# The scan of a time mix run over pairs of tokens instead of single tokens

## What is computed

```python
def step(S, ins):
    r_t, k_t, v_t, w_t = ins
    kv = jnp.einsum('bhi,bhj->bhij', k_t, v_t)
    y_t = jnp.einsum('bhi,bhij->bhj', r_t, S + u[None, :, :, None] * kv)
    return (w_t[..., None] * S + kv, y_t)
...
x = _layernorm(x + time_mix(x))
x = _layernorm(x + experts(x))
```

## Time and profile before

| what | us |
|---|---|
| median of 3 runs (lowest, highest) | 2341.41 (2340.97, 2342.73) |
| profiled execution, its own time | 2343.03 |
| its span | 2341.3 |
| busy: PE, DVE, ACT, POOL | 1938.1, 1834.2, 1059.1, 1373.3 |
| first scan, last scan starts | 65.6, 1274.7 |
| mean granted TensorE clock | 0.922 |

### The profile page before, as it was taken

One profiled execution on the slowest core, in us unless ns is written; L12 is line 12 of the kernel. 1 busy time (PEld: TensorE's weight loads), 2 busy tenths in 40 slices (PEclk: granted clock), 3 DMA queues, 4 the chain that ended last, 5 costly groups with the idle time before them and its releaser, 6 DMA issues. The chain is left out here.

```text
span 2341.3 us, 33041 instructions
## 1 busy us (share of the span) xinstructions
PE 1938.1 (83%) x9894; PEld 1336.8 (57%) x9894; DVE 1834.2 (78%) x3157; ACT 1059.1 (45%) x1919; POOL 1373.3 (59%) x954
## 2 busy tenths in 40 slices
PE   5777888788777887877776299999999999999980
PEld 2333343333333333433332189999999999999970
DVE  2899999899999998999997266666666666666655
ACT  2233553345334543444432255555555555555546
POOL 3667787768777787678775224444444444454440
PEclk9889999899989998999886599999999999999995
DMA  6932111111112111111020144545454545455538
GB/s 163 220 87 64 46 46 54 47 54 36 51 47 58 29 51 42 58 29 49 31 69 20 58 122 121 122 121 120 120 120 122 120 120 121 120 123 122 124 57 287
DMA packets 172844, 209.00 MB, mean 89 GB/s; under 512 B 12796, under 2 KB 152480, under 8 KB 172768
## 3 DMA queue, kind: packets, MB, share of 16 engines
q1 hardware_dynamic: 112688, 143.09, 20.7%
q0 software_dynamic: 28672, 34.78, 8.6%
q10 hardware_dynamic: 31408, 30.33, 5.0%
HBM read 118.65 MB, written 75.53 MB: 83 GB/s over the span
## 5 line engine op out<-in xcount | busy, mean ns | idle before, releaser
L807 DVE TENSOR_TENSOR_SCAN S<-wT,S,vb 128x512 f32<-128x512 f32 x512 | 624.9, 1262 | 0.0
L1070 POOL TENSOR_TENSOR prod<-S,rT 128x2048 f32<-128x2048 f32 x128 | 536.8, 4198 | 148.0 <-DVE S L807 147.8
L1289 PE MATMUL up<-x_parts,w_parts 128*128 128x308 f32 x3072 | 464.2, 307 | 1.5 <-DVE x_parts L1402 1.5
L1304 PE MATMUL down<-w_parts,h_parts 128*128 128x512 f32 (+1 forms) x1280 | 452.4, 396 | 0.0
L1289 PEld LDWEIGHTS up<-x_parts,w_parts 128*128 128x128 f32 x3072 | 439.2, 189 | 4.1 <-issue 1.8
L1364 POOL TENSOR_TENSOR ye<-ye,weight 128x256 f32<-128x256 f32 (+1 forms) x160 | 197.7, 1235 | 379.9 <-DVE ye L1458 379.9
L1342 ACT ACTIVATE h_full<-up,b_now 128x616 f32<-128x616 f32 x256 | 198.6, 776 | 421.2 <-PE up L1289 409.6
L1372 POOL DMA_INDIRECT sums<-ye,sum_at x160 | 281.6, 1760 | 150.1 <-POOL ye L1364 140.0
L1445 DVE TENSOR_TENSOR h_parts<-h_full,h_parts 128x616 fp32r<-128x616 f32 x256 | 206.8, 808 | 193.1 <-ACT h_parts L1342 192.8
L1307 PE MATMUL down<-w_parts,h_parts 128*128 128x256 f32 (+1 forms) x1280 | 357.4, 279 | 0.0
L571 PE MATMUL vb<-v_stack,pick_v 128*128 128x512 f32 x512 | 216.7, 507 | 152.0 <-DVE S L807 151.8
(11 more groups left out here) (176 smaller groups left out, 2645.2 us busy)
## 6 DMA issues: line engine op xcount, KB each, us to landing
w_raw<-in_L_ffn_w_dram SPq DMA_DIRECT2D x64, 1024.0 KB, 8.8
expert_in_rows<-y_tok ACTq DMA_DIRECT2D x30, 652.5 KB, 9.1
xe<-expert_in_rows SPq DMA_DIRECT2D x32, 522.0 KB
v_stack<-v_parts SPq DMA_DIRECT2D x64, 256.0 KB, 4.5
x_tok<-in_L_attn_x_dram SPq DMA_DIRECT2D x16, 512.0 KB, 3.3
x_res<-in_L_attn_x_dram SPq DMA_DIRECT2D x16, 512.0 KB, 3.4
sums<-x_row SPq DMA_DIRECT2D x16, 512.0 KB, 2.9
rows<-sums SPq DMA_DIRECT2D x16, 512.0 KB, 5.5
```

The source lines that it names most:

```text
L807: dve.tensor_tensor_scan(line[:, 1:TC + 1], wT[:, par, half, :], vb[:, p % 2, g, :], line[:, 0:1], ALU.mult, ALU.add).then_inc(scanned, 1)
L1070: pool.tensor_tensor(prod[:, q % 2], S[:, q % RING, :, 0:TC], rT[:, par, half, None, :].to_broadcast([P, QUAD, TC]), ALU.mult).then_inc(pr ...
L1289: last = pe.matmul(up[:, f % 2, half, 0:HC], w1_parts[:, par, wp, k, f * P:(f + 1) * P], x_parts[:, par, xp, k, half * HC:(half + 1) * HC] ...
L1304: pe.matmul(down[0:m, (par * TILES + t) % 2, :, :], h_parts[:, 0, f, t * P:t * P + m], w2_parts[:, par, :, f, :], start=f == 0, stop=False)
```

## The change

The recurrence is run over pairs of tokens. For an even token e and the odd token o behind it, S(o) = w(e) w(o) S + [w(o) k(e) v(e) + k(o) v(o)], so the scan takes 256 steps of w_pair = w(e) w(o), and its input is the sum of two products. The even token's output is r(e) times the state before the pair. The odd token's is r(o) w(e) times the same state, plus a term of its own, r(o) k(e) summed over the head's channels, times v(e). In each chunk the even tokens are put first and the odd ones behind them, in every tile; DMAs of x and x1 read and write the rows in that order, and the counting matmuls keep the order of tokens with a second triangular matrix, `upto`. xp is a new tile that holds, for each token, x of the token before it. `last_norm` puts four neighbouring rows on a partition.

```diff
-              "B0": 27, "B1": 28}
+              "B0": 26, "B1": 27, "D0": 28, "D1": 29}
-        LATER = {"hid": 3, "V": 3, "B": 3}
+        LATER = {"hid": 3, "V": 3, "B": 2, "D": 2}
+        def in_pairs(dram, first):
+            return dram[bass.ds(first, TC), :].rearrange("(l p b) c -> p b l c", p=P, b=2)
...
 @@ PE
+                    if s == AT[f"D{h}"]:
+                        a_fill(i, f"D{h}")
+                        pe.wait_ge(next_done, stage_value(i, 1, 1))
+                        pe.matmul(pa_of(f"D{h}")[:, 0:TP], sum_head[:].rearrange("p j h -> p (j h)"), r_next[:, h, :],
                                   start=True, stop=True).then_inc(a_full, 1)
...
-                    pe.matmul(ypsum[:], ident[:], uT[:, par, half, :], start=False, stop=True).then_inc(y_full, 1)
+                    pe.matmul(ypsum[:], ident[:], uT[:, par, half, :], start=False, stop=False)
+                    wait_drained(pe, i, f"D{half}")
+                    pe.matmul(ypsum[:, TP:TC], ident[:], uT_next[:, par, half, :], start=False, stop=True
+                              ).then_inc(y_full, 1)
...
 @@ DVE
+                    if s == AT[f"D{h}"] + LATER["D"]:
+                        dve.wait_ge(a_full, stage_value(i, NA, FA[f"D{h}"] + 1))
+                        dve.tensor_tensor(uT_next[:, par, h, :], pa_of(f"D{h}")[:, 0:TP], v_full[:, h, 0:TP], ALU.mult
+                                          ).then_inc(drained_sem(f"D{h}"), 1)
...
                     if p == 0:
-                        wait_drained(dve, i, "R1")
-                        dve.wait_ge(w_done, stage_value(i, NH, NH))
-                    for g in range(2):
-                        dve.wait_ge(vb_full, stage_value(i, NU, 2 * p + g + 1))
-                        dve.tensor_tensor(vb[:, p % 2, g, :], vb[:, p % 2, g, :], kT[:, par, half, :], ALU.mult
-                                          ).then_inc(kv_done, 1)
+                        dve.wait_ge(folded, stage_value(i, 3, 3))
+                    dve.wait_ge(vb_full, stage_value(i, NU, 2 * p + 2))
+                    even, odd = vb[:, p % 2, :, 0:TP], vb[:, p % 2, :, TP:TC]
+                    dve.tensor_tensor(kv_even[:], even, kT[:, par, half, None, 0:TP].to_broadcast([P, 2, TP]), ALU.mult
+                                      ).then_inc(kv_done, 1)
+                    dve.tensor_tensor(odd, odd, kT[:, par, half, None, TP:TC].to_broadcast([P, 2, TP]), ALU.mult
+                                      ).then_inc(kv_done, 1)
+                    dve.wait_ge(kv_done, stage_value(i, NU, 2 * p + 2))
+                    dve.tensor_tensor(even, odd, kv_even[:], ALU.add).then_inc(kv_summed, 1)
                     if p % 2 == 0:
                         dve.wait_ge(start_set, stage_value(i, NQ, q + 1))
+                    dve.wait_ge(kv_summed, stage_value(i, NPAIR, p + 1))
                     for g in range(2):
                         line = S[:, q % RING, 2 * (p % 2) + g, :]
-                        dve.wait_ge(kv_done, stage_value(i, NU, 2 * p + g + 1))
-                        dve.tensor_tensor_scan(line[:, 1:TC + 1], wT[:, par, half, :], vb[:, p % 2, g, :],
+                        dve.tensor_tensor_scan(line[:, 1:TP + 1], w_pair[:, par, half, :], vb[:, p % 2, g, 0:TP],
                                                line[:, 0:1], ALU.mult, ALU.add).then_inc(scanned, 1)
...
 @@ ACT
-                        act.activation(xT[:, h, 1:TC + 1], pa_of(f"x{h}"), ACT.Copy).then_inc(drained_sem(f"x{h}"), 1)
+                        now = pa_of(f"x{h}")
+                        act.activation(xp[:, h, TP:TC], now[:, 0:TP], ACT.Copy)
+                        act.activation(xp[:, h, 1:TP], now[:, TP:TC - 1], ACT.Copy)
+                        act.activation(xT[:, h, :], now, ACT.Copy).then_inc(drained_sem(f"x{h}"), 1)
...
 @@ POOL
+                if s == AT["R1"] + 1:
+
+                    pool.wait_ge(rk_done, stage_value(i, NH, NH))
+                    pool.tensor_tensor(r_next[:], rT[:, par, :, TP:TC], kT[:, par, :, 0:TP], ALU.mult
+                                       ).then_inc(next_done, 1)
+                    pool.wait_ge(next_done, stage_value(i, 1, 1))
+                    pool.wait_ge(w_done, stage_value(i, NH, NH))
+                    pool.tensor_tensor(kT[:, par, :, 0:TP], kT[:, par, :, 0:TP], wT[:, par, :, TP:TC], ALU.mult
+                                       ).then_inc(folded, 1)
+                    pool.tensor_tensor(w_pair[:, par], wT[:, par, :, 0:TP], wT[:, par, :, TP:TC], ALU.mult
+                                       ).then_inc(folded, 1)
+                if s == AT["R1"] + 2:
+                    pool.wait_ge(next_done, stage_value(i, 1, 1))
+                    pool.tensor_tensor(rT[:, par, :, TP:TC], rT[:, par, :, TP:TC], wT[:, par, :, 0:TP], ALU.mult
+                                       ).then_inc(folded, 1)
...
-                pool.tensor_tensor(prod[:, q % 2], S[:, q % RING, :, 0:TC],
-                                   rT[:, par, half, None, :].to_broadcast([P, QUAD, TC]), ALU.mult
-                                   ).then_inc(prod_done, 1)
+                pool.tensor_tensor(prod[:, q % 2].rearrange("p g (b s) -> p g b s", b=2),
+                                   S[:, q % RING, :, None, 0:TP].to_broadcast([P, QUAD, 2, TP]),
+                                   rT[:, par, half, :].rearrange("p (b s) -> p b s", b=2)[:, None]
+                                   .to_broadcast([P, QUAD, 2, TP]), ALU.mult).then_inc(prod_done, 1)
...
 @@ last_norm
-            return dram[bass.ds(g * (GT * P) + first, GT * P), :].rearrange("(t p) c -> p t c", p=P)
+            return dram[bass.ds(g * (GT * P) + first, GT * P), :].rearrange("(p t) c -> p t c", t=GT)
```

More of the change, by code:

```diff
@@ L176, in time_mix @@
         uT = sb("uT", [P, 2, NH, TC])
+        w_pair = sb("w_pair", [P, 2, NH, TP])
+        r_next = sb("r_next", [P, NH, TP])
+        uT_next = sb("uT_next", [P, 2, NH, TP])
+        kv_even = sb("kv_even", [P, 2, TP])
         v_parts = sb("v_parts", [P, 2, NH, TC], F32R)
         v_stack = sb("v_stack", [P, 2, NH, 2, TC], F32R)
-        S = sb("S", [P, RING, QUAD, TC + 1])
+        S = sb("S", [P, RING, QUAD, TP + 1])
         carry = sb("carry", [P, NQ, QUAD])
@@ L248, in time_mix @@
         rk_done = sem("rk_done")
+        next_done = sem("next_done")
+        folded = sem("folded")
+        kv_summed = sem("kv_summed")
         vb_full = sem("vb_full")
@@ L461, in stage_a @@
                     for h in range(NH):
-                        pe.matmul(pa_of("hid"), w1_sb[:, h, :], xT[:, h, 1:TC + 1], start=h == 0, stop=False)
+                        pe.matmul(pa_of("hid"), w1_sb[:, h, :], xT[:, h, :], start=h == 0, stop=False)
                     for h in range(NH):
-                        last = pe.matmul(pa_of("hid"), w1_before[:, h, :], xT[:, h, 0:TC], start=False,
+                        last = pe.matmul(pa_of("hid"), w1_before[:, h, :], xp[:, h, :], start=False,
                                          stop=h == NH - 1)
@@ L556, in stage_c @@
                     for t in range(TPC):
-                        pe.matmul(pc[:, t * E:(t + 1) * E], ones[:], seen[:], start=True, stop=False)
-                        for b in range(t):
-                            pe.matmul(pc[:, t * E:(t + 1) * E], ones[:], hits[:, b, :], start=False, stop=False)
-                        last = pe.matmul(pc[:, t * E:(t + 1) * E], before[:], hits[:, t, :], start=False, stop=True)
+                        b, l = t // 2, t % 2
+                        to = pc[:, t * E:(t + 1) * E]
+                        pe.matmul(to, ones[:], seen[:], start=True, stop=False)
+                        for done in range(l):
+                            for side in range(2):
+                                pe.matmul(to, ones[:], hits[:, 2 * side + done, :], start=False, stop=False)
+                        pe.matmul(to, upto[:] if b else before[:], hits[:, l, :], start=False, stop=False)
+                        last = pe.matmul(to, before[:], hits[:, 2 + l, :], start=False, stop=True)
                     last.then_inc(c_full, 1)
@@ L682, in stage_a @@
                     wait_from(dve, a_full, stage_value(i, NA, 0))
-                    dve.tensor_tensor(xx[:], xT[:, :, 0:TC], xT[:, :, 1:TC + 1], ALU.subtract).then_inc(xx_done, 1)
+                    dve.tensor_tensor(xx[:], xp[:], xT[:], ALU.subtract).then_inc(xx_done, 1)
                 for f, n in enumerate(DVE_MIXES):
@@ L1055, in stage_a @@
                                 pool.wait_ge(weighed, stage_value(i, MIX * NH - NSHORT, f * NH + h + 1 - NSHORT))
-                            pool.tensor_tensor(m, m, xT[:, h, 1:TC + 1], ALU.add).then_inc(mixed, 1)
+                            pool.tensor_tensor(m, m, xT[:, h, :], ALU.add).then_inc(mixed, 1)
                 for h in range(NH):
```

34 lines of the change are left out of this document (20 added, 14 removed).

## The result

The changed kernel takes 2397.11 us (median of 4 runs, 2391.85 to 2403.86) against 2341.81 (2340.97 to 2342.73) for the kernel before on the same chip: ratio 1.0238, 95% interval 1.0211 to 1.0264. It is 2.4% slower, where 2344 us was forecast within 2308 to 2372. The profiled execution has a span of 2396.2 us, 54.9 above that of before. The first rows are from the page of the changed kernel: its busy times, then its groups (busy, mean ns | idle before).

What follows compares the result with a forecast made beforehand. GpSimd was taken to hold stretch A in six chunks and a three-engine loop to end stretch B, VectorE not bounding alone. Chunk gains and losses, prologue +5 and end -0.5 summed to +2.5 us: 2344 us, range 2308 to 2372.

Steps and rivals of the forecast that it cites:

- hidden in the 6.75 us that GpSimd idles before the product of group 7: GpSimd's four added 128x512 products a chunk, 1.27 us each, 5.1 us together, were to cost nothing in its idle time.
- the slower rival on the product's own price: GpSimd's product of S and r gets dearer with half lines, up to 0.9 us each; say 2365 us; chance 0.15.
- stretch A: Chunk 2, last scans to first K matmul, 208.0 to 239.3 (31.3 us); set by GpSimd in six chunks, no gain there.
- the chunks after a branch: Chunks 5, 7, 9, 11, 13: VectorE sets stretch A, with 3.4 us of room; it gains 1.7 us there.
- Pair: VectorE's two products, their sum and two 256-step scans take 3.30 us instead of 3.54, saving 0.24 us.
- B0's drain: Moved ahead of pair 14, which then waits for spread, B0 and uT product: 2.3 us instead of 0.5, +1.75 us.
- stretch C: Chunk 2, spread of pair 14 to last scan's end, 271.4 to 282.8 (11.4 us); forecast +1.6 us.
- D0's and D1's drains: VectorE's new drains of the D matmuls; D0's beside B1's in front of pair 15; +0.36 us each.
- Prologue +5: Before the first scan: VectorE waits for the fourth fold, +3.3 us, and ScalarE's copies add 1.6: +5 us.
- Chunk 0: VectorE sets this chunk; 16 x 0.24 us saved, less two D drains: -3 us.
- Chunk 15: VectorE sets this chunk; forecast -3.8 us.
- two signs of being wrong: Last scans of two chunks under 74 us apart on the whole, or the product's mean over 4.3 us.

Runs made afterwards that it cites:

- The pair alone: Kernel before with only the changed kernel's VectorE pair (w in place of w_pair) and its product of S and r: 2331.92 us, ratio 0.997.
- the best variant: Changed kernel with group 6's product behind the top-2 chain, D matmuls late, xT shifted one word and folds by halves: 2355.63 us, ratio 1.0067.

## Why the prediction was wrong

**The step that failed:** "They stand between the second r*k product and the product of group 6, and are hidden in the 6.75 us that GpSimd idles before the product of group 7." GpSimd's idle time did take them: its wait before group 7 is down from 6.75 to 5.45 us in chunk 2. It was forecast to be nearly gone; it stayed because VectorE had become later itself. But I had asked only who waits for GpSimd's results, not what runs on VectorE while the product runs. Moved by 5.1 us, the product of group 6 covered the top-2 chain. That is +28.5 us by the run that takes only this away, and +60 by the run that adds only this to the kernel before. No rival had it; the slower rival on the product's own price had the right engine and the wrong quantity, since the mean stayed at 4.19 us.

**A second step failed by a smaller sum:** the x additions, which I took at their old price without naming them as touched. They cost 0.18 us more each; the run with x shifted is 9 us faster.

Point by point:
- That GpSimd holds stretch A in six chunks: right. After the change K starts 0.05 to 0.15 us behind GpSimd's additions in all eight, and with scans of half the length it still stands at 30.9 us in chunk 8. That it stands at 31.0 there both before and after is luck, as said above: chunks 2, 3 and 4 show 0.7 to 0.9 us more. In the chunks after a branch K moved from 32.9 to 33.9 us up to 32.0, 0.8 to 1.9 us where 1.7 was forecast.
- Pair: 0.24 us saved was forecast, and chunk 15 shows one pair every 3.41 us (1271.37 to 1274.78), so 0.13. Of the 0.11 us between the forecast pair of 3.30 and this, 0.05 are the two scans (0.735, taken at 0.71) and the rest gaps around the sum. The pair alone brings 9 us.
- B0's drain, +1.75 us in stretch C: right in size (1.6 in chunk 8). D0's and D1's drains, priced at 0.36 us: 0.33 each. For the D matmuls' wait for B's drain I had no term; TensorE stood 70.0 us in 14 chunks for it. Half of that was the hold again (35.5 us with the product behind the chain), and VectorE waited only 5.9 us for spreads, so most of it cost nothing. The run with D's matmuls late puts this wait and B0's drain together at 8 us once the hold is gone, not at 14 times 1.75: without the drain pair 14 waits for its spread.
- Prologue +5: VectorE's first product starts at 70.40 us in place of 64.36, +6.0. The second r*k product ends 2.8 us later, where I had 1.6 for ScalarE's copies; the four folds take the forecast 5.1, and the D drains are done 2 us before them. Chunk 0 from there: -1.1 where -3 was forecast. Chunk 15: -3.8 forecast, -0.1 found, as its pair saves half and VectorE waited 2.4 us for spreads.
- I had named two signs of being wrong: last scans under 74 us apart, and a mean of the product over 4.3 us. Neither came (80 us, 4.19 us), and the forecast was wrong all the same: both signs tested the rivals that I had thought of.

**How the range failed:** its upper end, 2372, came from prices of the new operations. That an operation moved into idle time can hold another engine had no term at all.

What stays open: the 13 us between the best variant and the kernel before, 10.6 in the two profiled executions. By the marks they are +7.3 to the first scan, -5.4 in chunk 0, +4.9 in the chunks 1 to 14, +1.8 in chunk 15 and +2.1 behind it. Their causes I did not separate. Candidates are the three copies of x on ScalarE in place of one, with 12.7 us of waits of VectorE's xx for them, and the wait for `rstd`, 22.9 us against 11.4, in which a faster pair may only arrive earlier. No variant was faster than the kernel before; the pair alone is, by 0.3%, but it is only a part of the change.

## What to carry to other kernels

Before idle time of GpSimd is called free, list what VectorE runs in the window to which the next long GpSimd operation moves: a 0.15 us step with two SBUF inputs, or a small cast, can become 4.1 us, and appears as a long instruction, not as a wait. Put such short chains ahead of the product, if need be with a wait on GpSimd. And before an engine's largest item is shortened, measure what its absence would bring: here 264 us of VectorE's work were worth 60.

## What the runs showed of the hardware

- A subtraction of 128x4 (0.15 us when alone) lasted 0.2 to 4.14 us beside a product on GpSimd that had started 0.1 to 4.0 us before, and ended 0.02 to 0.04 us after it, in the changed kernel and in five of the runs. A cast of 128x8 with one SBUF input was held too (4.05 us). The products of vb (PSUM) with kT, the scans, MAX8 and FIND_INDEX8 ran beside such products at their usual length.
- It goes the other way too: GpSimd operations of at most 128x8 that take 0.18 to 0.24 us lasted 1.05 to 1.25 us beside VectorE's `xx` (128x1024, two SBUF inputs) and ended 0.05 to 0.06 us after it, in eight chunks of the kernel before.
- The same GpSimd addition of two 128x512 tiles takes 1.27 us, or 1.09 us when one of them starts at word 1 of a tile that is one word longer.
- TensorE's first R matmuls take 1.98 us at a granted clock of 1.00 and 3.36 us at 0.59, after nearly the same idle time of some 1.5 us.
